# Fetching a transformer kernel's input rows by index from POOL instead of by one transfer from SP

## What is computed

```python
x = L0_attn_x                                        # (4, 1024, 128) float32
x = x + 0.5 * _L0_ffn_ref(_layernorm(x), ...)        # 4 experts, the best one by token
x = x + _L0_attn_ref(_layernorm(x), ...)             # 16 heads, causal
x = x + 0.5 * _L0_ffn_ref(_layernorm(x), ...)
x = x + 0.5 * _L1_ffn_ref(_layernorm(x), ...)        # 8 experts, the best two by token
x = x + _L1_attn_ref(_layernorm(x), ...)             # softmax and a second weighting
x = x + 0.5 * _L1_ffn_ref(_layernorm(x), ...)
```

## Time and profile before

| what | value |
|---|---|
| median of 3 runs | 3367.01 us (3366.42 to 3370.7) |
| the profiled execution's own time | 3365.29 us |
| its span, first to last instruction | 3363.5 us |
| busy share PE / DVE / ACT / POOL | 85% / 83% / 73% / 55% |
| mean granted TensorE clock | 0.947 of full speed |
| first block | 0 to 17.93 us |

### The profile page before, as it was taken

One profiled execution on the slowest core, in us unless ns is written; L12 is line 12 of the kernel. 1 busy time (PEld: TensorE's weight loads), 2 busy tenths in 40 slices (PEclk: granted clock), 3 DMA queues, 4 the chain that ended last, 5 costly groups with the idle time before them and its releaser, 6 DMA issues. The chain is left out here.

```text
span 3363.5 us, 65180 instructions
## 1 busy us (share of the span) xinstructions
PE 2852.9 (85%) x19634; PEld 1232.4 (37%) x19824; DVE 2785.2 (83%) x5044; ACT 2456.3 (73%) x3005; POOL 1834.0 (55%) x1027
## 2 busy tenths in 40 slices
PE   3985999999989789758888888888888888884799
PEld 3763444444367645422222222222222222222555
DVE  5997777777479866669999999999999999996665
ACT  3982556656568555329999999999999999993454
POOL 3210000000022245409999999999999999994354
PEclk9996999999979889869999999999999999997799
DMA  3002111011000000020000000000000000000000
GB/s 93 1 0 97 33 33 35 32 34 34 10 1 0 0 1 1 0 87 14 12 14 11 14 11 14 11 14 11 14 11 14 11 14 11 14 4 1 4 10 13
DMA packets 50313, 62.18 MB, mean 18 GB/s; under 512 B 9808, under 2 KB 29264, under 8 KB 50224
## 3 DMA queue, kind: packets, MB, share of 16 engines
q1 hardware_dynamic: 50224, 61.08, 5.8%
HBM read 45.60 MB, written 14.68 MB: 18 GB/s over the span
## 5 line engine op out<-in xcount | busy, mean ns | idle before, releaser
L1396 POOL TENSOR_TENSOR a_sg<-a_sg,a_shifted 128x1664 f32<-128x1664 f32 x256 | 955.7, 3733 | 21.3
L1593 DVE TENSOR_REDUCE a_mx<-a_pm 128x1 f32<-128x1024 f32 x512 | 619.8, 1211 | 21.1 <-PE a_pm L1435 21.0
L1602 DVE TENSOR_SCALAR a_sg<-a_pa 128x1024 int32<-128x1024 int32 x512 | 619.8, 1211 | 4.4 <-PE a_pa L1435 4.1
L1515 ACT ACTIVATE a_pt<-a_pb 128x1024 f32<-128x1024 f32 x512 | 524.3, 1024 | 108.9 <-PE a_pb L1435 108.9
L1452 PE MATMUL a_po<-a_pt,a_Vh 128*32 128x512 f32 x2048 | 539.3, 606 | 2.2 <-ACT a_sg L1534 2.2
L1452 PE MATMUL a_po<-a_sg,a_Vh 128*32 128x512 f32 x2048 | 539.3, 606 | 0.0
L1287 DVE TENSOR_REDUCE a_mx<-a_pm 128x1 f32<-128x512 f32 (+3 forms) x768 | 404.4, 550 | 158.1 <-PE a_pm L1126 150.0
L1214 ACT ACTIVATE a_pt<-a_pb 128x512 f32<-128x512 f32 (+3 forms) x768 | 337.3, 500 | 268.5 <-PE a_pb L1140 96.9
L1393 POOL TENSOR_SCALAR a_shifted<-a_sg,a_parh 128x1664 f32<-128x1664 f32 x256 | 470.3, 1837 | 101.9 <-DVE a_sg L1602 63.9
L1530 ACT ACTIVATE a_sg<-a_sg,a_parh 128x2048 f32<-128x2048 f32 x256 | 512.0, 2000 | 0.0
L1534 ACT ACTIVATE a_sg<-a_sg 128x2048 f32<-128x2048 f32 x256 | 489.9, 1914 | 0.0
(11 more groups left out here) (241 smaller groups left out, 5775.1 us busy)
## 6 DMA issues: line engine op xcount, KB each, us to landing
all_Q<-q_parts SPq DMA_DIRECT2D x384, 48.0 KB
all_K<-k_parts SPq DMA_DIRECT2D x384, 48.0 KB
q_parts<-p_parts SPq DMA_DIRECT2D x16, 384.0 KB, 2.6
k_parts<-p_parts SPq DMA_DIRECT2D x16, 384.0 KB, 2.6
all_Q<-a_rows SPq DMA_DIRECT2D x192, 2.0 KB
out_dram<-all_X SPq DMA_DIRECT2D x8, 256.0 KB, 2.3
sw_raw<-in_f_We_dram SPq DMA_DIRECT2D x1, 1024.0 KB, 7.1
all_Q<-a_rows SPq DMA_DIRECT2D x64, 6.0 KB
```

Of the source, the lines that this page charges most:

```text
L1396: nc.gpsimd.tensor_tensor(buf[:, :, 0:CUT], buf[:, :, 0:CUT], shifted[:], ALU.mult)\
L1515: nc.scalar.activation(pt[(j - LT) % 4][:, i, :], pb[:], ACT.Exp, scale=SC)\
L1593: nc.vector.tensor_reduce(mx[:, (j // PER) % 2, t:t + 1], pm[:], AX.X, ALU.max)\
L1602: nc.vector.tensor_scalar(sg[(j - LS) % 4][:, i, :].bitcast(I32), pa[:].bitcast(I32), SIGN_OFF, None, ALU.bitwise_and).then_inc(abs_done, 1)
```

## The change

The one transfer of `X` from SP is taken out. POOL gets a part in the first block: it fills an index table `place` (128 partitions x 32 integers, entry [p, k] = 128 k + p) with one iota, waits for it, and issues 32 indirect transfers, each of which fetches 128 rows of 512 bytes to one tile of `X` by the 128 indices of one column of the table. Then POOL waits until all 32 have landed. SP's list is one shorter and its wait at the block's end counts three transfers.

```diff
@@ -1672,18 +1672,30 @@
+        place = m.sb("place", [P, NT], I32)
+        placed, gathered = m.sem("placed"), m.sem("gathered")
+        x_rows = x.rearrange("b t d -> (b t) d")
         with nc.Block() as block:
+
+            @block.gpsimd
+            def _(pool):
+                nc.gpsimd.iota(place[:], [[P, NT]], base=0, channel_multiplier=1).then_inc(placed, 1)
+                pool.wait_ge(placed, 1)
+                for k in range(NT):
+                    nc.gpsimd.indirect_dma_start(X[:, k, :], None, x_rows,
+                                                 bass.IndirectOffsetOnAxis(ap=place[:, k:k + 1], axis=0))\
+                        .then_inc(gathered, 16)
+                pool.wait_ge(gathered, 16 * NT)
 
             @block.sync
             def _(sp):
-                sp.dma_start(X[:], x_v).then_inc(loaded, 16)
                 sp.dma_start(ident[:], w["ident"]).then_inc(loaded, 16)
...
-                sp.wait_ge(loaded, 64)
+                sp.wait_ge(loaded, 48)
```

## The result

| what | before | changed |
|---|---|---|
| median of 3 runs | 3367.01 us | 3389.55 us (3386.76 to 3391.27) |
| ratio of the runs | | 1.0068, 95% interval 1.0054 to 1.0082 |
| span of the profiled execution | 3363.5 us | 3387.8 us |
| next block starts at | 17.93 us | 46.20 us |
| first use of X at | 38.09 us | 63.73 us |

The account below looks back on a forecast made before the run. SP's 24 issues were taken to bound the first block; 32 gathers at 1.20 us, landing and block step move its end from 17.93 to 42.1 us. That +24.1 us on 3367.0 us gives 3391.1 us, range 3372 to 3420 us.

Parts of the forecast that it names:

- first gather starts: First block, POOL's list: after the index table's iota and its semaphore wait, 0.3 us, the first gather at 1.1 us.
- last gather's end to the wait's end: End of POOL's list: the last gather's 64 KB land some 2.1 us after its issue ends, as with SP's transfers.
- rest of the kernel: From the third stage on: same instructions, only later; 2 us either way allowed for shifted clock dips and the runs.
- SP's saving: First block, SP's list without X's issue and the 5.30 us stall behind it: 5.8 us shorter, through at 11.7 us.
- The price of a gather: First block, POOL: 1.20 us per gather, taken from a 512-column subtraction; bounds 0.47 and 1.84 us.
- The block's end: Step from the first block's end to the next block's first instruction: 0.45 us, as in the kernel before.
- The second block: Raw-weight block after the first: content unchanged, gain from quieter loading at most 2.4 us, taken as 0.
- Rival 1: First block: each gather waits for the previous landing, 2.4 us each, +60 us, 3427 us; chance 0.12 with a milder form.
- Rivals 2 and 3: First block: gathers at 0.28 to 0.66 us, no measurable difference (0.10); or under 0.28 us, faster (0.02).
- rival 2: First block: a gather nearly as cheap as SP's issue, 0.28 to 0.66 us, total 3361 to 3374 us; chance 0.10.

## Why the prediction was right, and what was off in it

The forecast was 3391.1 us, +24.1 us; measured were 3389.55 us, +22.5 us. The mechanism was the one named: POOL's list takes the place of SP's as the end of the first block, and nothing behind the block absorbs it. The profiled executions differ by 24.3 us in span, and the terms, predicted and found, are:

| term | predicted | found |
|---|---|---|
| first gather starts | 1.1 us | 1.67 us |
| from there to the last gather's end | 38.4 us | 39.9 us |
| last gather's end to the wait's end | 2.1 us | about 1.5 us |
| from there to the next block | 0.45 us | about 3.1 us |
| next block starts | 42.1 us | 46.2 us |
| second block, shorter by | 0 (at most 2.4) | 2.6 us |
| rest of the kernel | 0 (2 either way) | -1.3 us |

So 4.1 us too little in the first block were made up by 4.0 us too much behind it. That the sum comes within 1.6 us is luck: two errors of 4 us cancel.

- *SP's saving.* Right in size: its list ends at 11.6 us, 11.7 us were said, and 5.30 us became 0.42 us.
- *The price of a gather.* 1.20 us was taken, 1.25 us measured. The number was right and the reason for it was not. The prediction counted 512 numbers to be written for 128 rows, one index at a time. The runs with 64 and 16 rows show that the rows cost nearly nothing, and the run with plain transfers shows that issuing the same rows costs 0.53 us. What is paid is a fixed price for the indexed form, and 0.30 of its 1.25 us are gaps, where no gaps were expected. That a 512-column subtraction takes the same time is a coincidence.
- *The block's end.* "The step from a block's end to the next block's first instruction is 0.45 us" was carried over from a block in which POOL had issued nothing. It is the step that was mis-sized, by the DRAIN of 2.68 us, and no row of before could show it.
- *The second block.* "I take 0" was too low, and the bound of 2.4 us just too narrow. The mechanism given for it was right for 1.5 us of it; most of the rest arises at the second raw weight, for a reason that stays open.
- *Rival 1,* gathers one after another: excluded by starts 1.25 us apart with 0.30 us between, while the last one's landing takes 1.5 us more after its own end. The Trainium skill ("DMA: Bandwidth & Descriptors", "Anatomy of one DMA — SWDGE (gpsimd) path") calls most of its 2.0 us completion and the generation of descriptors "small, variable". The trace agrees that part of a gather is completion, 1.5 us that the next gathers overlap; the cost that decides here is the issue, 1.25 us each.
- *Rivals 2 and 3,* a cheap gather: not met for gathers. Plain transfers from POOL are that case. At 0.53 us each they lie between the 0.28 and 0.66 us of rival 2, and 3369.98 us lies in its 3361 to 3374 us; the DRAIN and the wait for landing put the next block at 23.13 us.
- *A reading.* The dips of the clock in the earlier trace rows are in the fourth slice, from the twelfth to the eighteenth (the text says nineteenth) and in two near the end. Nothing in the sum hangs on it.

## What to carry to other kernels

A gather costs POOL 1.25 us per instruction, 1.15 us when it has an eighth of the rows, and a plain transfer 0.53 us; multiply by the count and ask whether POOL's list is then the longest in its block. In this chain of blocks that starts with loads, the first block was ended by the longest list of issues, and by the landings once that list was shortened; merging it with the next block gained 7 us and stopped where the DMA engines were busy throughout. Of a row that happens to have the right duration, ask whether what it scales with is what the new operation scales with.

## What the runs showed of the hardware that was not expected

- POOL's DRAIN at a block's end takes about 0.06 us plus 0.082 us for each transfer that POOL issued in the block: 0.14, 1.37 and 2.68 us after 1, 16 and 32, the same for plain and indexed transfers, with 16 and with 128 rows, and with 14 us of other POOL work in between.
- An indexed transfer is held up by DVE: the five gathers that met a DVE instruction of 1.6 to 2.3 us with two SBUF inputs ended 0.82 us after it and took up to 2.90 us instead of 0.94 us.
- Behind a transfer of 2 MB in rows of 512 bytes the next issue in SP's queue took 5.3 us (6.2 us with ACT issuing beside it); behind the same 2 MB in 32 transfers, 0.43 us.
